# Metaformer block with routed experts: the last weight transfer in 80 and 5 partitions, and index searches in pairs ahead of the up products

## The chip, the cores and the metric

The kernel runs on one core of a Trainium2 chip. The metric is device time in microseconds of one execution; lower is better. The profile is one execution recorded by the hardware profiler. TensorE multiplies matrices, VectorE (DVE), ScalarE (ACT) and GpSimd (POOL) work elementwise, SyncE (SP) only issues transfers, as ScalarE and GpSimd do on the side.

## The reference, cut to what matters

```python
x = x + conv1x1(layernorm_over_channels(x), W)      # x: (16, 128, 16, 16), W from 32 reflections
t = tokens(x)                                       # 4096 tokens of 128 channels
xf = layernorm(t)
Sm = softmax(xf @ W_router + b_router)              # 32 experts
G_ek, idx_ek = top_k(Sm.T, 128)                     # each expert takes its 128 best tokens
tokens = xf[idx_ek]                                 # gather
act = silu(tokens @ W_up[group] + b_up[group])      # 8 groups of 4 experts, 341 columns
Eout = act @ W_down[expert] + b_down[expert]
y = zeros.at[idx_ek].add(G_ek[..., None] * Eout)    # scatter-add
x = from_tokens(t + y)
```

## The kernel before

**Front half.** The 4096 tokens are worked on in 8 chunks of 512 (`CH`), 4 tiles of 128 each. TensorE transposes and mixes, VectorE and ScalarE take the statistics, GpSimd scales the logits and the softmax. The normalised tokens `xf` and the softmax rows `S` are stored side by side in HBM as `token_rows`, the residual `x1` in a first accumulator `acc0`, and a second, `acc1`, is filled with zeros. Then each expert's threshold is searched and a 0/1 selection `sel` made of it, with prefix counts `cum`.

**Index searches.** `find(e)` (L1099) is one small TensorE product that picks, for the 128 slots of expert e, the rows of `cum` in which the slots' tokens lie. `token_number(e)` on VectorE (L904, L906) counts in this row and writes `idx[:, e]`. Two PSUM banks take turns, so `find(e)` waits for index e - 2. After every fourth index VectorE makes one more `onehot` (L898, L899). Eight searches (`FIRST_FINDS`) are made before the first up product. The other 24 are spread by two functions that say how many must have been made ahead of up product j of unit k and ahead of the down products of expert e: TensorE calls both, and VectorE follows the same order in its loop over the experts, where `find_up_to` and `while found < finds_before_down(e)` stand.

**Experts.** The 32 experts run in 9 units of 2, 2, 4, 4, 4, 4, 4, 4, 4. GpSimd gathers one expert's 128 rows with an indirect DMA (L493), as soon as its index is there and once all stores of `token_rows` and of both accumulators have landed. TensorE transposes a unit's rows (L1117), multiplies them with `wup` in three up products (L1129), ScalarE applies SiLU (L620), and TensorE multiplies with `wdn` (2 x 128 rows) and `wdn2` (85 rows and the bias) in three steps per expert (L1142). VectorE scales the result by the gate (L945). Order on TensorE: up(0), then for each unit k up(k + 1), the transposes of unit k + 2, down(k).

**Way back.** All gathers stand ahead of the scatters in GpSimd's queue, since `AHEAD = E`. The first 26 experts' outputs are scattered with adding DMAs (L502), alternately into `acc0` and `acc1`; each waits for the last one into the same accumulator. The last 6 experts (`ON_PE`) are added by TensorE instead: VectorE splits the outputs into three bf16 parts (L920 to L923) and makes a one-hot of the tokens (`hot`, L914), and 144 products (L1164) add them up in all eight PSUM banks. Then both accumulators are read back (L429 on SyncE's queue, L624 on ScalarE's), summed by VectorE (L953), transposed by TensorE into the same banks (L1169), copied by ScalarE (L627) and stored (L432).

**SyncE's queue**, in order: V, constants, x, more constants, `wup` (L400), `bup`, `wdn` in two transfers (L404), `wdn2` (L405), the down bias (L406), the zero fill of `acc1` (L410), then for each chunk the store of `x1` (L414) and of `S` (L417), the stores of `xf` (L423) in the order 0, 7, 1, 2, 3, 4, 6, 5, and after the first index the 1 MB load of the column numbers (L426).

Of the kernel before, what the change touches and what calls it, by code (L numbers as in the profile page):

```python
# [20 lines left out]
ROW = C + E  # L21
FF = [(0, 128), (128, 128), (256, DFF - 256)]
FR = DFF - 256
LEVELS = HH.bit_length() - 1
FLOOR = 2.0 ** -102

# [49 lines left out]


def finds_before_up(k, j):
    downed = UNITS[k - 1][0] if k else 0
    return min(E, FIRST_FINDS + downed + 3 * k + j + 1)  # L80


def finds_before_down(e):
    ups = 3 * min(UNIT_OF[e] + 2, len(UNITS))
    return min(E, FIRST_FINDS + e + ups + 1)


def constants():
# [32 lines left out]
def metaformer_block(nc, x, V, w_router, b_router, w_up, b_up, w_down, b_down, c32, c16, ch16, ccol, out):  # L121
# [7 lines left out]
    with ctx:  # L129
# [261 lines left out]
        @block.sync  # L391
        def _(sp):
            sp.dma_start(v_raw[:, :], V).then_inc(s_v, 16)
            sp.dma_start(k32[:, 0:2 * P], c32[:, 0:2 * P]).then_inc(s_const, 16)
            sp.dma_start(k32[:, 2 * P:C32_COLS], c32[:, 2 * P:C32_COLS]).then_inc(s_merge, 16)
            for g in range(CH):
                sp.dma_start(X[:, g, :].rearrange("p (u n) -> p u n", u=TPC), x_v[g // 2, g % 2]).then_inc(s_x[g], 16)
            sp.dma_start(k16[:, :], c16).then_inc(s_const16, 16)
            sp.dma_start(kh16[:, :], ch16).then_inc(s_const16, 16)
            sp.dma_start(wup[:, :, :], w_up.rearrange("g c f -> c g f")).then_inc(s_wup, 16)  # L400
            for j, (f0, fn) in enumerate(FF):
                sp.dma_start(bup[0:fn, j, :], b_up[f0:f0 + fn, :]).then_inc(s_bup, 16)
            for j in range(2):
                sp.dma_start(wdn[:, :, j, :], w_down[:, j * P:(j + 1) * P, :].rearrange("e f c -> f e c")).then_inc(s_wdn, 16)  # L404
            sp.dma_start(wdn2[0:FR, :, :], w_down[:, 2 * P:DFF, :].rearrange("e f c -> f e c")).then_inc(s_wdn, 16)  # L405
            sp.dma_start(wdn2[FR:FR + 1, :, :], b_down.rearrange("(o e) c -> o e c", o=1)).then_inc(s_wdn, 16)  # L406

            sp.wait_ge(s_zero, 1)
            for q in range(4):
                sp.dma_start(acc[1][q * 1024:(q + 1) * 1024, :].rearrange("(p k) c -> p (k c)", p=P), zero[:, :]).then_inc(s_acc1, 16)  # L410
            for g in range(CH + 2):
                if g < CH:
                    sp.wait_ge(s_x1, TPC * (g + 1))
                    sp.dma_start(acc_v[0][g], per_chunk(x1, g)).then_inc(s_acc0, 16)  # L414
                if g >= 2:
                    sp.wait_ge(s_S, g - 1)
                    sp.dma_start(rows_v[g - 2, :, :, C:ROW], per_chunk(S, g - 2)).then_inc(s_rows_s, 16)  # L417
            for g in (0, CH - 1, 1, 2, 3, 4, CH - 2, 5):
                if g < CH - 2:
                    sp.wait_ge(s_xf, g + 1)  # L420
                else:
                    sp.wait_ge(s_xfp, CH - g)
                sp.dma_start(rows_v[g, :, :, 0:C], per_chunk(xf, g)).then_inc(s_rows_x, 16)  # L423

            sp.wait_ge(s_idx, 1)
            sp.dma_start(columns, ccol.to_broadcast([P, TOK])).then_inc(s_col, 16)  # L426
            sp.wait_ge(s_sc[0], 16 * INTO.count(0))
            for g in range(CH):
                sp.dma_start(per_chunk(y0, g), acc_v[0][g]).then_inc(s_y[g], 16)  # L429
            for g in range(CH):  # L430
                sp.wait_ge(s_yo, g + 1)
                sp.dma_start(out_v[g // 2, g % 2], yo[:, g, :].rearrange("p (u n) -> p u n", u=TPC)).then_inc(s_out, 16)  # L432
            sp.wait_ge(s_out, 16 * CH)

        @block.gpsimd
        def _(pool):
# [73 lines left out]
            for e in range(AHEAD):  # L510
                gather(e)
            e = 0
            while AHEAD + 2 * e < E:
                scatter(e)
                gather(AHEAD + 2 * e)
                gather(AHEAD + 2 * e + 1)
                e += 1
            while e < SCATTERED:
                scatter(e)
                e += 1  # L520
# [435 lines left out]
        def _(pe):  # L956
# [146 lines left out]
            def find_up_to(n):  # L1103
                while finds[0] < n:
                    find(finds[0])
                    finds[0] += 1
# [24 lines left out]
            def down(k):  # L1131
                e0, n = UNITS[k]
                pe.wait_ge(s_act, 3 * (k + 1))
                for q in range(n):
                    e = e0 + q
                    find_up_to(finds_before_down(e))
                    if e >= 3:
                        pe.wait_ge(s_eo, e - 2)
                    for j in range(3):
                        w = wdn[:, e, j, :] if j < 2 else wdn2[:, e, :]  # L1140
                        rows_ = P if j < 2 else FR + 1
                        ins = mm(down_bank(e), act[0:rows_, k % 2, j, q * P:(q + 1) * P], w, start=(j == 0), stop=(j == 2))  # L1142
                    ins.then_inc(s_dn, 1)

            pe.wait_ge(s_wup, 16)
            pe.wait_ge(s_wdn, 64)
            gathered_transpose(0)
            up(0)
            gathered_transpose(1)
# [40 lines left out]
```

## Time and profile before

| | us |
|---|---|
| median of 3 runs | 200.35 |
| lowest and highest | 199.31, 201.8 |
| the profiled execution, as timed | 198.85 |
| its span, first to last instruction | 196.8 |

In the span TensorE's matmuls are busy 146.2 us (74%), weight loads 89.2, GpSimd 108.4 (55%), VectorE 91.1, ScalarE 71.0. About 2 us of the profiled execution lie outside its span. The mean granted TensorE clock is 0.809 of full speed. Busy shares are means over stages with different limits; what a stage waits for has to be read from its own stretch.

### The profile page before, as it was taken

Reading aid. Unit: us, or ns where it says so; the run is one execution under the profiler, and the core shown is the slowest. Engines: PE = TensorE matmul, PEld = TensorE weight load, DVE = VectorE, ACT = ScalarE, POOL = GpSimd, SP = SyncE. Lnnn points to the kernel's source line nnn. Section 1 sums busy time; section 2 is a strip of 40 time slices with the busy share of each in tenths; the row PEclk is TensorE's granted clock in tenths of the full one; section 3 lists DMA queues with packets and bytes.
Section 4 is the critical chain, followed back from the end, with each engine's and each line's share of the span. In section 5 each row is a group of like instructions: output and inputs, shape, how many; then the busy total and the mean of one; then the engine's idle time right before and its main releaser. Section 6 shows DMA issues by size and latency. Waiting matters only on the chain.

```text
span 196.8 us, 2406 instructions
## 1 busy us (share of the span) xinstructions
PE 146.2 (74%) x697; PEld 89.2 (45%) x697; DVE 91.1 (46%) x407; ACT 71.0 (36%) x241; POOL 108.4 (55%) x118
## 2 busy tenths in 40 slices
PE   1999965723126213995999699999975999999990
PEld 0557855611105101452357236776662344444590
DVE  2454998984774861322464513221299022200550
ACT  3266999437894500321233132345400000000161
POOL 2027479986460027773766557687788778730000
PEclk9999998555555555557599859999996699999999
DMA  4999994336989952221212122243414333369996
GB/s 98 301 336 308 289 292 120 82 81 214 393 252 263 330 217 67 67 70 33 66 51 67 33 70 32 27 40 27 40 17 40 27 27 34 35 113 328 395 284 189
DMA packets 33502, 28.31 MB, mean 144 GB/s; under 512 B 6800, under 2 KB 27216, under 8 KB 33360
## 3 DMA queue, kind: packets, MB, share of 16 engines
q1 hardware_dynamic: 26769, 21.70, 37.5%
q0 software_dynamic: 5280, 4.33, 15.3%
q10 hardware_dynamic: 1440, 2.13, 3.3%
q8 instruction: 6, 0.10, 0.2%
q14 instruction: 7, 0.06, 0.1%
HBM read 17.53 MB, written 10.62 MB: 143 GB/s over the span
## 4 chain that ended last, share of the span: by engine, by line
PE 37%; POOL 21%; issue 14%; DVE 12%; DMA 9%; ACT 3%; another core or an unknown queue 1%; SPq 0%; POOLq 0%; DVEq 0%; ACTq 0%
POOL acc L502 8%; PE PT L1129 7%; PE PZ L1142 6%; PE PM L1129 6%; POOL rs L463 4%; DMA x<-acc 3%; PE PM L1142 3%; POOL rs L456 3%; PE PT L969 3%; DMA acc<-X,idx 2%; PE PZ L1169 2%; PE PT L1117 2%; POOL act L469 2%; DVE wdn L914 2%; POOL act L466 2%
## 5 line engine op out<-in xcount | busy, mean ns | idle before, releaser
L502 POOL DMA_INDIRECT acc<-X,idx x26 | 43.4, 1669 | 11.5 <-issue 9.3
L493 POOL DMA_INDIRECT xg<-token_rows,idx x32 | 30.5, 954 | 31.4 <-DVE idx L906 23.2
L904 DVE TENSOR_SCALAR_CACHE_REDUCE junk<-PZ,k 128x128 f16<-128x128 f32 x32 | 11.1, 347 | 24.8 <-PE PZ L1099 14.6
L1017 PE MATMUL PZ<-stage_w,X 128*128 128x192 f32 x64 | 16.2, 410 | 6.3 <-DVE act L749 5.8
L1142 PE MATMUL PZ<-wdn,act 128*128 128x128 f32 x132 | 18.2, 281 | 1.0 <-DVE X L945 1.0
L627 ACT ACTIVATE X<-PZ 128x512 f32<-128x512 f32 x4 | 2.4, 597 | 45.2 <-PE PZ L1169 45.2
L1129 PE MATMUL PT<-xgT,wup 128*128 128x512 f32 (+3 forms) x28 | 18.2, 740 | 0.0
L620 ACT ACTIVATE act<-PT,bup 128x512 f32<-128x512 f32 (+3 forms) x14 | 9.0, 640 | 24.3 <-PE PT L1129 20.9
L1017 PEld LDWEIGHTS PZ<-stage_w,X 128*128 128x128 f32 x64 | 13.4, 238 | 8.2 <-DVE act L749 7.4
L1142 PEld LDWEIGHTS PZ<-wdn,act 128*128 128x128 f32 x132 | 16.0, 191 | 2.4 <-DVE X L945 1.4
L1129 PE MATMUL PM<-xgT,wup 128*128 128x512 f32 (+3 forms) x26 | 16.2, 714 | 0.0
L1164 PE MATMUL PZ<-wdn,S 128*128 128x512 bf16 x48 | 14.6, 410 | 2.1 <-DVE X L945 2.1
L1099 PE MATMUL PZ<-cum,onehot 32*128 32x129 f16 x32 | 8.0, 258 | 9.2 <-DVE idx L906 4.2
L945 DVE TENSOR_SCALAR X<-PZ,xg 128x128 f32<-128x128 f32 x22 | 7.6, 349 | 15.0 <-PE PZ L1142 12.5
L620 ACT ACTIVATE act<-PM,bup 128x512 f32<-128x512 f32 (+3 forms) x13 | 8.3, 636 | 16.7 <-PE PM L1129 13.6
L914 DVE TENSOR_SCALAR wdn<-wide,slot_token 128x4096 bf16<-128x4096 f16 x6 | 7.8, 1302 | 13.7 <-PE PZ L1164 13.7
L1099 PEld LDWEIGHTS PZ<-cum,onehot 32*128 32x128 f16 x32 | 3.0, 96 | 22.8 <-issue 16.2
L558 ACT ACTIVATE act<-act,mn 128x32 f32<-128x32 f32 x32 | 9.8, 309 | 5.8 <-DVE mn L753 5.8
L953 DVE TENSOR_TENSOR x<-x,xf 128x512 f32<-128x512 f32 x8 | 5.2, 692 | 14.3 <-DMA x<-acc 14.2
L712 DVE SCALAR_TENSOR_TENSOR x<-PZ,rs,xg 128x128 f32<-128x128 f32 x32 | 9.1, 347 | 4.0 <-PE PZ L1017 2.4
L1117 PE MATMUL PT<-k,xg 128*128 128x128 f32 x32 | 6.4, 328 | 5.5 <-DMA xg<-token_rows,idx 5.5
L1117 PEld LDWEIGHTS PT<-k,xg 128*128 128x128 f32 x32 | 5.1, 174 | 10.8 <-issue 10.8
(172 smaller groups left out, 280.5 us busy)
## 6 DMA issues: line engine op xcount, KB each, us to landing
X<-in_x SPq DMA_DIRECT2D x8, 256.0 KB, 5.2
acc<-zero SPq DMA_DIRECT2D x4, 512.0 KB, 5.2
acc<-x SPq DMA_DIRECT2D x8, 256.0 KB, 4.2
token_rows<-xf SPq DMA_DIRECT2D x8, 256.0 KB, 3.6
xf<-acc ACTq DMA_DIRECT2D x8, 256.0 KB, 5.7
x<-acc SPq DMA_DIRECT2D x8, 256.0 KB, 7.2
out<-X SPq DMA_DIRECT2D x8, 256.0 KB, 3.1
wup<-in_L_ffn_W_up SPq DMA_DIRECT2D x1, 1364.0 KB, 7.8
```

The costliest lines, as they stand in the source:

```text
L493: nc.gpsimd.indirect_dma_start(out=xg[:, e, :], out_offset=None, in_=rows[:, :], in_offset=bass.IndirectOffsetOnAxis(ap=idx[:, e:e + 1], a ...
L502: nc.gpsimd.indirect_dma_start(out=acc[i][:, :], out_offset=bass.IndirectOffsetOnAxis(ap=idx[:, e:e + 1], axis=0), in_=eo[:, e, :], in_off ...
L558: ins = nc.scalar.activation(pr[:, g, u, :], lg[:, g, u, :], ACT.Exp, bias=mn[:, g, u:u + 1], scale=-1.0, accum_out=sm[:, g, u:u + 1])
L620: nc.scalar.activation(act[0:fn, k % 2, j, 0:n * P], src, ACT.Silu, bias=bup[0:fn, j, e0 // PER:e0 // PER + 1]).then_inc(s_act, 1)
L904: link(nc.vector.tensor_scalar(junk2[:, :], PZ[:, e % 2, 0:P], c_("slot_col"), None, ALU.is_le, ALU.add, accum_out=below[:, e:e + 1]))
L914: nc.vector.tensor_scalar(hot(k), columns, slot_token[:, k:k + 1], None, ALU.is_equal).then_inc(s_hot, 1)
L1017: ins = mm(PZ[:, 2 * (g % 2) + u // 2, (u % 2) * W_:(u % 2 + 1) * W_], X[:, g, u * P:(u + 1) * P], stage_w[:, :], start=True, stop=True)
L1099: mm(PZ[:, e % 2, 0:P + 1], onehot[r, g, :], cum[r, g, 0:P + 1], start=True, stop=True).then_inc(s_find, 1)
L1117: ins = nc.tensor.transpose(PT[:, 0, q * P:(q + 1) * P], xg[:, e0 + q, 0:C], ident)
L1129: mm(dst, wup[:, e0 // PER, f0:f0 + fn], xgT[:, k % 2, 0:n * P], start=True, stop=True).then_inc(s_up, 1)
L1142: ins = mm(down_bank(e), act[0:rows_, k % 2, j, q * P:(q + 1) * P], w, start=(j == 0), stop=(j == 2))
L1164: ins = mm(out_bank(g), parts[j][:, k, :], hot(k)[:, g * 512:(g + 1) * 512], start=(k == 0 and j == 0), stop=False)
```

## The change

`wdn2`'s 85 weight rows are loaded by two DMAs, of 80 partitions and of 5, where there was one; the semaphore that TensorE waits for counts one DMA more. Ahead of each up product stand two searches (after the first eight, until all 32 are made, which is ahead of the last up product of unit 3), and none between down products; VectorE's order follows through the same function. A loop on GpSimd that ran no time with `AHEAD = E` is removed.

```diff
+FR_EVEN = FR // 16 * 16
...
 def finds_before_up(k, j):
-    downed = UNITS[k - 1][0] if k else 0
-    return min(E, FIRST_FINDS + downed + 3 * k + j + 1)
+    return min(E, FIRST_FINDS + 2 * (3 * k + j + 1))
 
 
 def finds_before_down(e):
-    ups = 3 * min(UNIT_OF[e] + 2, len(UNITS))
-    return min(E, FIRST_FINDS + e + ups + 1)
+    return min(E, FIRST_FINDS + 6 * min(UNIT_OF[e] + 2, len(UNITS)))
...
-            sp.dma_start(wdn2[0:FR, :, :], w_down[:, 2 * P:DFF, :].rearrange("e f c -> f e c")).then_inc(s_wdn, 16)
+            for f0, f1 in ((0, FR_EVEN), (FR_EVEN, FR)):
+                sp.dma_start(wdn2[f0:f1, :, :], w_down[:, 2 * P + f0:2 * P + f1, :].rearrange("e f c -> f e c")).then_inc(s_wdn, 16)
...
-            while AHEAD + 2 * e < E:
-                scatter(e)
-                gather(AHEAD + 2 * e)
-                gather(AHEAD + 2 * e + 1)
-                e += 1
...
                     e = e0 + q
-                    find_up_to(finds_before_down(e))
                     if e >= 3:
...
-            pe.wait_ge(s_wdn, 64)
+            pe.wait_ge(s_wdn, 80)
```

## Rows read from the trace of the kernel before

**Rows 1.** Chain that ended last, its end: start us, us, what.
```profile
172.81 4.47 DMA acc<-X,idx
177.30 6.68 DMA x<-acc
184.75 2.22 PE PZ L1169 x16
```

**Rows 2.** Timeline of GpSimd: start us, us, engine, line, what, [idle before <-releaser].
```profile
72.20 1.22 POOL L493 DMA_INDIRECT xg<-token_rows,idx  x1 [14.65 <-DVE idx L906]
...
118.54 0.94 POOL L493 DMA_INDIRECT xg<-token_rows,idx  x1 [1.82 <-DVE idx L906]
119.79 1.62 POOL L502 DMA_INDIRECT acc<-X,idx  x1 [0.30 <-issue]
```

**Rows 3.** Busy time by stretch: length, then engines, granted clock, DMA share, GB/s.
```profile
89.70:92.00 2.30, 0.04 (x1) 0.07 (x1) 0.52 (x3) 0.08 (x1) 0.00 (x0) 0.78 0.13 36
92.00:98.10 6.10, 6.10 (x9) 1.82 (x10) 2.95 (x16) 1.37 (x2) 4.28 (x5) 0.52 0.18 46
...
108.90:110.70 1.80, 0.04 (x1) 0.07 (x1) 0.96 (x6) 0.00 (x0) 0.00 (x0) 1.00 0.18 46
110.70:117.60 6.90, 6.90 (x14) 2.35 (x14) 2.21 (x14) 2.16 (x4) 4.71 (x5) 0.56 0.24 59
...
150.30:155.50 5.20, 5.15 (x13) 1.82 (x14) 2.04 (x4) 0.00 (x0) 3.96 (x3) 0.50 0.30 25
155.50:184.30 28.80, 28.80 (x133) 12.78 (x131) 4.26 (x4) 0.00 (x0) 15.21 (x9) 0.99 0.56 124
```

**Rows 4.** Timeline, ScalarE and VectorE after their pauses.
```profile
89.18 0.60 ACT L611 ACTIVATE xgT<-PT 128x512 f32<-128x512 f32 x1 [1.98 <-remote]
91.27 0.35 DVE L904 TENSOR_SCALAR_CACHE_REDUCE junk<-PZ,k 128x128 f16<-128x128 f32 x1 [5.06 <-remote]
...
109.71 0.35 DVE L945 TENSOR_SCALAR X<-PM,xg 128x128 f32<-128x128 f32 x1 [2.05 <-PE PZ L1142]
```

**Rows 5.** Timeline, the last chunks of xf (ScalarE), a one-hot and the first index (VectorE).
```profile
52.69 7.79 ACT L590 ACTIVATE xf<-x,shift,rs 128x128 f32<-128x128 f32 x20
...
66.83 0.35 DVE L899 SCALAR_TENSOR_TENSOR onehot<-k,bend,after 128x128 f16<-128x128 f16 x1
...
67.48 0.15 DVE L906 SCALAR_TENSOR_TENSOR idx<-below,PZ 128x1 int32<-128x1 f32 x1
```

**Rows 6.** Timeline of SyncE's queue: how long an issue held it.
```profile
20.59 8.07 SPq L405 DMA_DIRECT2D wdn<-in_L_ffn_W_down  x1
28.71 15.92 SPq L406 DMA_DIRECT2D wdn<-in_L_ffn_b_down  x1
...
61.34 5.81 SPq L423 DMA_DIRECT2D token_rows<-xf  x8
```

**Rows 7.** Busy time by stretch, for the DMA: last two columns, share and GB/s.
```profile
32.00:44.00 12.00, 6.49 (x19) 5.21 (x19) 11.01 (x70) 6.25 (x38) 10.96 (x20) 0.54 0.37 82
48.00:52.00 4.00, 1.00 (x6) 0.54 (x5) 2.24 (x8) 3.07 (x12) 2.44 (x3) 0.50 1.03 394
```

**Rows 8.** The page, DMA issues: KB each, median us from issue to landing.
```profile
token_rows<-xf SPq DMA_DIRECT2D x8, 256.0 KB, 3.6
...
wide<-in_const_columns SPq DMA_DIRECT2D x1, 1024.0 KB, 6.1
...
xg<-token_rows,idx POOLq DMA_INDIRECT x32, 2.7
```

**Rows 9.** Chain of waits: up and down products at the full clock.
```profile
100.92 1.05 PE PM L1129 x2
...
105.99 0.86 PE PM L1142 x6
107.01 0.86 PE PZ L1142 x6
...
118.86 1.34 PE PZ L1142 x12
```

## The prediction

> **What bounds the kernel now.** I read the chain of waits first, from its end [rows 1]: the last scatter (L502) is issued at 172.81 and lands 4.47 later, the y loads follow from 177.30 and take 6.68, VectorE sums the first chunk, and TensorE turns sums into output from 184.75 on. GpSimd's timeline [rows 2] shows where that end comes from. Its 32 gathers are issued from 72.20 to 118.54, its 26 scatters from 119.79 to 172.81 [rows 1, 2]. A scatter every (172.81 - 119.79) / 25 = 2.12 us is its steady pace, and a gather takes 0.94 + 0.30 of issue, about 1.25 us: 31 steps of that are 38.8 us, while it took 46.3. So 7.5 us of the gather stretch is waiting for indices, and all gathers stand ahead of the first scatter.
>
> The windows of TensorE [rows 3] show a second chain that ends at the same moment. From 150.30 to 184.30 it is busy without a gap (34 us) in the 144 token products (L1164), and only then do the sums reach it [rows 1]. So a gain on GpSimd alone buys nothing: both chains have to move, and the smaller move counts. Upstream on TensorE there are two holes, 89.70 to 92.00 and 108.90 to 110.70, and each is followed by a stretch at a granted clock of 0.5 (the 1.2 GHz level). The second hole is reopened by a search: VectorE got the product it waited for at 109.71 only, and in the first it came back at 91.27, after 5.06 us of idleness [rows 4].
>
> Both chains begin with the first gather. Its index is there at 67.63 (67.48 + 0.15) [rows 5], yet it starts at 72.20. GpSimd also waits there for the stores of xf into token_rows, which SyncE issued from 61.34 to 67.15 [rows 6], one behind the other. ScalarE had the last of these chunks ready at 60.48 [rows 5]. The SyncE queue was late: the transfer of 85 partitions at L405 and the small one behind it held it from 20.59 to 44.63 [rows 6]. From 32 to 44 the DMA engines moved 82 GB/s at a share of 0.37, and from 48 to 52, with ordinary transfers, 394 GB/s at 1.03 [rows 7]: the 85 partitions were spread over about a third of the engines.
>
> **The change part by part.** *The transfer in 80 and 5 partitions.* Nothing waits for wdn2 itself, its first reader is a down product, long after it has landed; what counts is the queue behind it. It is 85 x 32 x 512 B = 1.39 MB, 17 us at 82 GB/s. At the other rate of [rows 7] the 1.31 MB of 80 partitions take 3.3 us; twice that is my upper bound, since small packets may go slower. The 80 KB of the last 5 partitions take 1.0 us at the old rate. One more issue costs SyncE about 0.5 us. I expect 17 us to become 5 to 8, 6.5 as the middle, so SyncE is free about 10.5 us earlier, at 34 instead of 44.6. The fills and x1 stores then run while the channel statistics are computed, and the xf stores are no longer queued but go out as chunks come ready, the last at about 60.5. With 3.6 us to land [rows 8] it is there at 64 to 65, ahead of the index at 67.63. The first gather then waits for that index alone and starts at 67.9: 4.3 us earlier. Here the cover is 3 us thick; if it were gone, the start would move by less.
>
> The Trainium skill ("DMA: Bandwidth & Descriptors", section "Why a DMA increments its semaphore by 16 and not by 1") says that such a transfer uses the largest number of engines up to 16 that divides its outer size. That gives 5 for 85, 16 for 80, and 5 for the rest, and the share of 0.37 agrees. Its "Rules for kernel authors" say of two transfers to disjoint partition halves that they serialize and are not worth splitting; by that rule alone the queue would be no earlier, which is the second rival below.
>
> There is a new collision. The 1 MB load of the columns (L426) waits for index 0 and so starts just after 67.63 either way, and took 6.1 us to land; the first gathers now go out beside it, where they used to find it nearly done. A gather lands in 2.7 us [rows 8]. The second one, now issued at 69.4, lands at 72.1 undisturbed, and with the rest of that load (2.6 us at 394 GB/s) ahead of it at 73.8. I take 72.7, near the first since both are interleaved. Before, it was issued at 73.7 and landed at 76.4, and TensorE's first transpose waits for it, so TensorE's chain moves by 3.7 us (bounds 2.6 to 4.3).
>
> *Two searches ahead of each up product.* Before, 24 searches stand singly: one ahead of each of 15 up products and of 9 down groups. At the full clock a down group with a search takes 107.01 - 105.99 = 1.02 us, without one 1.34 / 2 = 0.67 [rows 9]: a lone search costs 0.35. Afterwards there are 12 pairs. The second of a pair costs at least 0 and at most another 0.35; I take 0.15, since it needs no switch of its own. 24 x 0.35 - 12 x 0.50 = 2.4 us at the full clock; as half of these places are at the low clock or hidden there, I take 1.5 us (bounds 0 and 3.1). VectorE must keep up: a search costs it 0.35 (L904 [rows 4]) and 0.15 (L906) and a short read between, so a pair about 1.1, and every second pair brings a one-hot (L899 takes 0.35 [rows 5], with its helper some 0.6). That is 1.4 on average. An up product at the full clock takes 1.05 [rows 9], with the pair ahead of it some 1.4 too: it fits, barely, and at the low clock easily.
>
> The indices now come in time for GpSimd. Index 31 is found in the 12th up product, about 97 to 99 us, and gather 31 at full pace goes out at 67.9 + 1.5 + 30 x 1.25 = 106.9. So the 7.5 us of waiting disappear, the first scatter starts at 108.2 instead of 119.8, and the last at 161.2 instead of 172.8. Experts' outputs are ready far ahead: those of the third unit were multiplied at 109.71 [rows 4]. GpSimd's chain moves by 11.6 us: 4.3 at the start, and 7.3 of the 7.5 (the first gather takes 0.3 longer than the others). Taking the gather loop's dead tail out changes no instruction.
>
> *No search between down products.* The hole at 108.90 was a search ahead of up product 12 that needed an index queued on VectorE behind the multiplications of the down results. After the change all searches are over by then, so its 1.8 us go, and with them the low clock after it. That price is seen at the late restart: 13 matmuls in 5.20 us against 133 in 28.80 [rows 3], 5.20 - 13 x 0.217 = 2.4 us. The hole at 89.70 is open: its releaser is not known to the profile ("remote"), ScalarE was held too, until 89.18 [rows 4], and the new order has all its searches done before the first down product, so VectorE's pause may be hidden, or fall inside the up products and be paid. Nothing (0) or 2.3 + 2.4 = 4.7 us is gained; the loss side is 2.7, the 5.06 us pause less the 2.3 already paid.
>
> **The sum.** TensorE: 3.7 + 1.5 + 1.8 + 2.4 = 9.4, plus 0.5 because the sums are there when it arrives, 9.9; with the first hole gone too, 14.6. GpSimd: 11.6. If TensorE gets ahead of GpSimd it idles 2 to 4 us before the sums, and the output stage starts at the low clock: 11.6 - 2.4 = 9.2. Both ways lead to about 9.5 us. The span of 196.8 becomes 187.3, the profiled execution's 198.85 becomes 189.35. The median of the runs, 200.35, lies 1.5 us above that execution, so the forecast is 200.35 - 9.5 = 190.85, say 190.9 us.
>
> **The rivals.** *Both holes come back, elsewhere.* For it: the first has no named releaser, so nothing shows that a search caused it. Against: all engines have more slack in the new order. TensorE then gains 3.7 + 1.5 + 0.5 = 5.7, and the time is 194.7. *The split does not free the queue*, because the two parts serialize or the b_down transfer behind them is what holds SyncE (L406 shows 15.92 us). Against it: that row is 16 KB and can only be waiting for what is ahead. The gather start stays at 72.2; the other terms give about 1.5 + 4.2 + 0.5 = 6.2 on TensorE and 7.3 on GpSimd, so 194.2. *Slower:* VectorE's pause of 5.06 us falls between two searches of a pair, TensorE idles in the middle of the up products, and the clock stays low through the up and down products after it, which were done at the full one. Each us of work at the full clock then costs another. Some 10 us of it would use up the gain, 14 us make the kernel slower by over 2%; 30 us of it would give over 215 us. Against it: the low stretches in [rows 3] are 5 to 7 us long, after holes of about 2 us. *More than forecast:* both holes vanish and the output stage starts at the full clock: 11.6, so 188.8.
>
> **How the numbers follow.** Forecast, 8 to 11 us saved: 0.58. The full 11.6: 0.10. Both holes: 0.16. Queue not freed: 0.07. Clock low, slower: 0.04. The remaining 0.05 is some wait not seen that eats most of the gain. A measurement of this kernel tells 2% from no change, 196.3 and 204.4. Forecast, full gain, both holes and queue lie below 196.3, 0.91 in all, of which I put 0.03 over the line for the scatter of the runs (199.31 to 201.8): 0.88 faster, 0.08 the same, 0.04 slower. The range reaches from the full gain, 188.8 less 0.8 of scatter, to the first rival's 194.7 plus as much: 188.0 to 195.5.
>
> **What would show it.** Right: L406 on the SyncE queue short and the fills starting near 34; the first gather at about 68; gathers every 1.25 us to about 107, with no wait for an index; the first scatter near 108; no TensorE hole before up product 12; the last scatter near 161; TensorE either unbroken into the output stage or idle for 2 to 4 us before it. Wrong: a first gather still after 70, gathers waiting for VectorE, a scatter pace above 2.3 us, or holes of over 2 us among the paired searches.

## The result, and the profile after

| | us |
|---|---|
| kernel before, median of 20 runs | 200.5 (199.25 to 204.23) |
| changed kernel, median of 20 runs | 201.42 (200.76 to 204.04) |
| ratio, 95% interval | 1.0075, 1.0049 to 1.0102 |
| profiled execution after: time, span, mean granted clock | 200.8, 198.5, 0.823 |

The change makes the kernel slower by 0.5 to 1.0%, where 190.9 was forecast. Some executions of any kernel fall into a slower state; here and below a ratio compares fast executions only, while a median is over all of them, so that the two can differ by 1%.

SyncE's queue, from its timeline in the changed kernel (start, how long it held the queue). The line numbers behind L404 are shifted: searches are L1094, up products L1124, transposes L1112, down products L1136, indices L899 and L901.

```profile
21.48 13.02 SPq L405 DMA_DIRECT2D wdn<-in_L_ffn_W_down  x2
34.54 0.32 SPq L406 DMA_DIRECT2D wdn<-in_L_ffn_b_down  x1
34.91 3.47 SPq L410 DMA_DIRECT2D acc<-zero  x4
...
52.55 9.18 SPq L423 DMA_DIRECT2D token_rows<-xf  x8
68.46 0.35 SPq L426 DMA_DIRECT2D wide<-in_const_columns  x1
```

L405 and L406 hold the queue until 34.86, where they held it until 44.63 [rows 6]. The stores of xf spread over 9.18 us since each waits for its chunk, and no longer queue behind one another.

GpSimd's timeline in the changed kernel:

```profile
69.36 1.22 POOL L493 DMA_INDIRECT xg<-token_rows,idx  x1 [10.95 <-DVE idx L901]
...
93.44 0.95 POOL L493 DMA_INDIRECT xg<-token_rows,idx  x1 [0.30 <-issue]
99.36 0.94 POOL L493 DMA_INDIRECT xg<-token_rows,idx  x1 [4.98 <-DVE idx L901]
...
108.86 0.94 POOL L493 DMA_INDIRECT xg<-token_rows,idx  x1 [2.33 <-DVE idx L901]
...
116.36 1.62 POOL L502 DMA_INDIRECT acc<-X,idx  x1 [0.30 <-issue]
```

The first gather is 2.84 us earlier than in [rows 2], and waits for the index alone. With it begins an unbroken run of twenty, one every 1.25 to 1.29 us after the first step, to 94.39. Then GpSimd waits twice for an index, 7.3 us in all: as much as before. The first scatter comes at 116.36, 3.4 us earlier than before, not 11.6.

ScalarE's and VectorE's timelines in the changed kernel, the idle time ahead of an instruction in brackets:

```profile
86.32 0.47 ACT L615 ACTIVATE act<-PT,bup 128x256 f32<-128x256 f32 x1 [3.78 <-PE PM L1124]
95.42 0.47 ACT L615 ACTIVATE act<-PM,bup 85x256 f32<-85x256 f32 x1 [8.62 <-remote]
97.56 0.60 ACT L606 ACTIVATE xgT<-PT 128x512 f32<-128x512 f32 x1 [1.68 <-remote]
...
118.84 0.69 ACT L615 ACTIVATE act<-PT,bup 128x512 f32<-128x512 f32 x1 [5.99 <-remote]
...
89.12 0.35 DVE L899 TENSOR_SCALAR_CACHE_REDUCE junk<-PZ,k 128x128 f16<-128x128 f32 x1 [4.37 <-remote]
```

And TensorE's:

```profile
81.66 1.22 PE L1124 MATMUL PT<-xgT,wup 128*128 128x256 f32 x2
83.48 0.27 PE L1094 MATMUL PZ<-cum,onehot 32*128 32x129 f16 x1 [0.60 <-issue]
...
85.09 1.15 PE L1124 MATMUL PM<-xgT,wup 128*85 128x256 f32 x2
86.04 1.06 PE L1112 MATMUL PT<-k,xg 128*128 128x128 f32 x4
86.89 2.76 PE L1136 MATMUL PZ<-wdn,act 128*128 128x128 f32 x12
98.22 0.36 PE L1094 MATMUL PZ<-cum,onehot 32*128 32x129 f16 x2 [8.56 <-ACT xgT L606]
...
119.58 1.09 PE L1124 MATMUL PT<-xgT,wup 128*85 128x512 f32 x2 [3.10 <-issue]
```

Set the two beside each other. The up product that ends at 82.88 is taken by ScalarE at 86.32; the one that ends at 86.24 at 95.42, 9.2 us later; the search of 83.48 is read by VectorE at 89.12, 5.4 us later. The transposes that end at 87.10 come last, at 97.56, 10.5 us later. ScalarE and VectorE were idle. By the profile TensorE's work was finished, but its readers went on only much later. I call such results late. The ends of matmuls are modelled in the profile, so it can't tell whether the product itself was late or only the word of it. The rows show that the delay grew from product to product (3.4, 5.4, 9.2, 10.5 us), and that the readers got the results in the order of TensorE's program. The releaser of four of the five waits in the first rows is put down to "remote", a source that the profile does not know, as in [rows 4]. TensorE runs ahead until it needs a copy of a late result, and then stands for 8.56 us.

The windows of the changed kernel, over both holes and the stretch between (columns as in rows 3):

```profile
89.65:98.22 8.57, 0.01 (x2) 0.01 (x1) 1.63 (x8) 1.07 (x2) 3.82 (x4) 0.50 0.19 48
98.22:104.60 6.38, 6.38 (x13) 1.99 (x14) 3.43 (x21) 1.37 (x2) 4.02 (x5) 0.52 0.15 39
116.50:119.58 3.08, 0.00 (x0) 0.00 (x0) 0.35 (x1) 0.74 (x2) 2.77 (x2) 1.00 0.34 48
```

Two holes are there again, and larger: 8.56 us against the first row of [rows 3], 3.08 against the third, though the second now stands ahead of the third up product of the unit, where it stood ahead of the first. The granted clock stays at its lower level (1.2 GHz) until about 104.6. In the end TensorE goes from its token products straight into the output stage at 187.16 (before: 184.75 [rows 1]), while the last scatter, at 169.66, is 3.15 us earlier than before. TensorE alone sets this end.

### The profile page after: what moved, and what is told of

The parts are those of the page before. It is cut to its first block, busy times and chain, and to the rows that moved or that the text cites. A ratio compares the mean times of both kernels' runs of the same rounds, so it can differ in the third digit from the quotient of the medians.

```text
span 198.5 us, 2410 instructions
## 1 busy us (share of the span) xinstructions
PE 139.5 (70%) x697; PEld 87.6 (44%) x697; DVE 91.0 (46%) x407; ACT 70.8 (36%) x241; POOL 109.2 (55%) x118
## 4 chain that ended last, share of the span: by engine, by line
PE 53%; POOL 13%; DVE 11%; issue 9%; another core or an unknown queue 5%; DMA 3%; ACT 3%; SPq 0%; POOLq 0%; DVEq 0%; ACTq 0%
PE PZ L1158 9%; PE PT L1124 7%; PE PZ L1136 6%; PE PM L1124 6%; PE PT L1158 4%; PE PM L1158 4%; POOL rs L463 4%; PE PM L1136 3%; POOL rs L456 3%; PE PT L964 2%; POOL act L469 2%; PE PZ L1163 2%; DVE wdn L909 2%; DMA k<-in_const_f 2%
## 5 line engine op out<-in xcount | busy, mean ns | idle before, releaser
L502 POOL DMA_INDIRECT acc<-X,idx x26 | 44.1, 1698 | 11.0 <-issue 7.5
L1012 PE MATMUL PZ<-stage_w,X 128*128 128x192 f32 x64 | 14.9, 385 | 6.9 <-DVE act L744 6.5
L1136 PE MATMUL PZ<-wdn,act 128*128 128x128 f32 x132 | 18.5, 289 | 1.0 <-DVE X L940 1.0
L1124 PE MATMUL PT<-xgT,wup 128*128 128x512 f32 (+3 forms) x28 | 17.0, 695 | 3.1 <-issue 3.1
L940 DVE TENSOR_SCALAR X<-PZ,xg 128x128 f32<-128x128 f32 x22 | 7.5, 349 | 23.1 <-PE PZ L1136 10.6
L1136 PEld LDWEIGHTS PZ<-wdn,act 128*128 128x128 f32 x132 | 17.2, 204 | 1.9 <-DVE X L940 1.4
L899 DVE TENSOR_SCALAR_CACHE_REDUCE junk<-PZ,k 128x128 f16<-128x128 f32 x32 | 11.1, 347 | 14.5 <-PE PZ L1094 7.3
L1094 PE MATMUL PZ<-cum,onehot 32*128 32x129 f16 x32 | 5.9, 263 | 16.7 <-ACT xgT L606 9.0
L1012 PEld LDWEIGHTS PZ<-stage_w,X 128*128 128x128 f32 x64 | 12.5, 226 | 8.3 <-DVE act L744 7.5
L1124 PE MATMUL PM<-xgT,wup 128*128 128x512 f32 (+3 forms) x26 | 15.2, 672 | 0.0
L1094 PEld LDWEIGHTS PZ<-cum,onehot 32*128 32x128 f16 x32 | 2.4, 97 | 26.5 <-issue 11.4
L463 POOL TENSOR_TENSOR rs<-ve,mhalf 128x4 f32<-128x4 f32 x8 | 8.1, 1006 | 4.0 <-DVE ve L729 4.0
L585 ACT ACTIVATE xf<-x,shift,rs 128x128 f32<-128x128 f32 x24 | 9.4, 482 | 0.0
L1003 PE MATMUL PM<-k,S 128*128 128x128 f32 x8 | 3.3, 408 | 8.4 <-ACT key L562 6.6
```

What stands on the lines that cost most here:

```text
L463: link(nc.gpsimd.tensor_tensor(rs2[:, g, :], ve2[:, g, :], mhalf[:, :], ALU.pow))
L502: nc.gpsimd.indirect_dma_start(out=acc[i][:, :], out_offset=bass.IndirectOffsetOnAxis(ap=idx[:, e:e + 1], axis=0), in_=eo[:, e, :], in_off ...
L585: ins = nc.scalar.activation(xf[:, t, :], x1[:, t, :], ACT.Identity, bias=shift2[:, g, u:u + 1], scale=rs2[:, g, u:u + 1])
L899: link(nc.vector.tensor_scalar(junk2[:, :], PZ[:, e % 2, 0:P], c_("slot_col"), None, ALU.is_le, ALU.add, accum_out=below[:, e:e + 1]))
L1012: ins = mm(PZ[:, 2 * (g % 2) + u // 2, (u % 2) * W_:(u % 2 + 1) * W_], X[:, g, u * P:(u + 1) * P], stage_w[:, :], start=True, stop=True)
L1124: mm(dst, wup[:, e0 // PER, f0:f0 + fn], xgT[:, k % 2, 0:n * P], start=True, stop=True).then_inc(s_up, 1)
```

## The experiments

The runs lay in five groups, each on another chip and at another time, so chip and time can't be told apart here. The kernel before took 200.36 us on chip A, 194.06 on B, 200.36 on C, 193.86 on D and 193.17 on E. Only kernels on one chip are set side by side; on which chip the runs of the result above lay is not known.

Two theories to begin with. **G**: a long unbroken run of indirect gathers on GpSimd makes TensorE's results late; before, waits for indices broke the run. **P**: the paired searches themselves stall TensorE and VectorE.

**The transfer alone** (chip A): the kernel before with only this.

```diff
-            sp.dma_start(wdn2[0:FR, :, :], ...
+            for f0, f1 in ((0, FR_EVEN), (FR_EVEN, FR)):
+                sp.dma_start(wdn2[f0:f1, :, :], ...
```

> The kernel before with the wdn2 transfer in 80 and 5 partitions, old order of the searches. Theory G (a long unbroken run of gathers holds back TensorE's results): the gathers start 3 us earlier, at 69.4, the indices come one per up product as before; the hole of 2.3 us near 90 stays or grows to 3 to 5 us, and the time is 197 to 200, a gain of 0.5 to 3 us. Theory P (the searches in pairs hold TensorE back): without pairs the hole is as before, the full shift of 2.8 us arrives, 197.5 to 198.

Measured: 197.1 us, ratio 0.9878 (0.9747 to 1.0009). ScalarE and TensorE at the first hole, from their timelines:

```profile
88.63 0.60 ACT L613 ACTIVATE xgT<-PT 128x512 f32<-128x512 f32 x1 [3.79 <-remote]
...
89.36 0.27 PE L1101 MATMUL PZ<-cum,onehot 32*128 32x129 f16 x1 [1.44 <-ACT xgT L613]
```

The first hole is 1.44 us. Here 14 gathers run from 68.74, then GpSimd waits 3.22 us for an index. But a second hole stands further on, larger than any of before:

```profile
120.94 0.69 ACT L622 ACTIVATE act<-PM,bup 128x512 f32<-128x512 f32 x1 [7.84 <-remote]
...
121.68 2.00 PE L1131 MATMUL PM<-xgT,wup 128*85 128x512 f32 x2 [4.60 <-ACT act L622]
```

ScalarE took at 120.94 an up product that ended at 116.22, behind seven unbroken gathers (107.33 to 115.79) and with two scatters already issued, at 116.09 and 118.02. Against the trace of before the first transpose starts 3.2 us earlier (73.25 and 76.47), but this execution, the slowest of the four, has only 1.0 us less span. The ratio stands for 2.4 us, and its interval just reaches no change.

**The order of the searches alone** (chip A).

```diff
-    return min(E, FIRST_FINDS + downed + 3 * k + j + 1)
+    return min(E, FIRST_FINDS + 2 * (3 * k + j + 1))
-    return min(E, FIRST_FINDS + e + ups + 1)
+    return min(E, FIRST_FINDS + 6 * min(UNIT_OF[e] + 2, len(UNITS)))
...
-                    find_up_to(finds_before_down(e))
```

> The kernel before with the new order of the searches, the transfer undivided; the gathers start at 72.2 as before and run without a break. Theory G: 20 gathers in one go, as in the changed kernel, so the same hole of about 8 us among the third unit's products, and 203 to 205, slower than before by the 2.8 us that the split brought to the changed kernel. Theory P: the same, so this run alone tells only whether the order and not the transfer makes the hole; if neither is right and the early transfers cause it, the hole is 2 us and the time 194 to 198.

Measured: 205.79 us, ratio 1.0353 (1.0205 to 1.0501). ScalarE's timeline:

```profile
87.29 0.47 ACT L618 ACTIVATE act<-PM,bup 128x256 f32<-128x256 f32 x1 [5.13 <-PE PT L1127]
94.38 0.47 ACT L618 ACTIVATE act<-PT,bup 128x256 f32<-128x256 f32 x1 [6.61 <-issue]
...
100.09 0.60 ACT L609 ACTIVATE xgT<-PT 128x512 f32<-128x512 f32 x1 [2.39 <-remote]
```

Late results again, behind 18 unbroken gathers (71.70 to 94.19). So the loss of the change is in the order: by the ratios the transfer gives 2.4 us (from a gain of 5.1 to a loss of 0.2) and the order costs 7.1 (4.1 to 10.0). The two together lost 0.9 to 1.8 us where results were late; the intervals are too wide to say whether the parts simply add. Both theories expect a loss here; the next runs tell them apart.

**Gathers of experts 8 to 31 left out** (chip A), so their rows hold what was in the buffer; the searches stay paired.

```diff
+GATHERED = 8
-            for e in range(AHEAD):
+            for e in range(GATHERED):
...
-                pe.wait_ge(s_g[k], 16 * n)
+                if e0 < GATHERED:
+                    pe.wait_ge(s_g[k], 16 * n)
```

> The changed kernel with the gathers of experts 8 to 31 left out (these experts multiply what lies in the buffer; all else is done). GpSimd is idle from about 80 on until the first scatter. Theory G: no late results on ScalarE and VectorE after 82, TensorE goes through the up and down products without the hole of 8.6 us and without the one of 3.1, and the clock comes back early; span 180 to 188. Theory P: the paired searches are all there, so the hole at 90 stays at 6 us or more.

Measured: 182.03 us. Windows of this kernel:

```profile
84.00:90.00 6.00, 6.00 (x25) 3.99 (x23) 2.79 (x16) 1.62 (x4) 3.10 (x2) 0.68 0.12 11
90.00:98.00 8.00, 7.92 (x43) 4.74 (x43) 4.86 (x29) 4.20 (x7) 3.17 (x3) 1.00 0.28 25
```

TensorE has no hole, with every pair of searches in place. P falls. This is one execution, and its time is no gain, since 24 gathers are missing.

**Gathers held until unit k - 2 is transposed** (chip A), which breaks the run by real waits.

```diff
             for e in range(AHEAD):
+                if UNIT_OF[e] >= 3:
+                    pool.wait_ge(s_gTs, UNIT_OF[e] - 1)
                 gather(e)
```

> The changed kernel, but the gathers of unit k (from the fourth unit on) wait until unit k - 2 has been transposed, which breaks their run into bursts of four. Theory G: the hole shrinks from 8.6 us to under 3, and the time is 190 to 197. Theory P: pacing changes nothing for TensorE, the hole stays, and the gathers end later: 201 to 205.

Measured: 200.26 us, ratio 0.9988 (0.9914 to 1.0062). GpSimd and ScalarE, from their timelines in the profiled execution, the fastest of ten at 197.34:

```profile
79.96 0.94 POOL L495 DMA_INDIRECT xg<-token_rows,idx  x1 [1.33 <-ACT xgT L608]
...
87.21 0.94 POOL L495 DMA_INDIRECT xg<-token_rows,idx  x1 [2.55 <-ACT xgT L608]
...
106.21 0.94 POOL L495 DMA_INDIRECT xg<-token_rows,idx  x1 [2.48 <-ACT xgT L608]
...
116.31 0.69 ACT L617 ACTIVATE act<-PT,bup 128x512 f32<-128x512 f32 x1 [5.48 <-remote]
```

With runs of 8, 4, 4, 4, 4 gathers the first hole is gone (ScalarE never idle over 2.2 us up to 90). But the pace is lost in waits, and the last eight gathers, 106.21 to 116.27 and almost unbroken, bring late results back. A run of eight at 68.62 had brought none, so no fixed number of gathers explains it.

**Plain transfers in place of gathers, from GpSimd's and from SyncE's queue** (chip B): experts 8 to 31 get fixed rows, as many bytes, so their tokens are other ones.

```diff
-                gather(e)
+                if e < 8:
+                    gather(e)
+                else:
+                    pool.wait_ge(s_idx, e + 1)
+                    nc.gpsimd.dma_start(xg[:, e, :], rows[e * P:(e + 1) * P, :]).then_inc(...)
```

> The changed kernel, but the rows of experts 8 to 31 are fetched from GpSimd's queue by plain transfers of the same 82 KB each, at fixed rows, when the index is ready (what these experts multiply is not what the reference asks for; the amount is the same). If it is the bytes landing in the buffer that hold TensorE's results back, the hole stays at 6 to 9 us. If it is the run of indirect issues on GpSimd, it goes or shrinks under 3 us, and the span is 182 to 190.

> As the run with plain transfers from GpSimd, but issued by SyncE, so GpSimd stands idle from the eighth gather to the first scatter, and the bytes still land in the same buffer. Bytes: hole of 6 us or more, span over 193. GpSimd's issues: no hole, span 178 to 184, as with the gathers left out (179.9).

Measured: 181.9 and 181.51 us, neither with a hole. I first read this as "not the bytes, but the gathers". Then the next two ran beside them, and the reading had to wait.

**Fewer gathers ahead** (chip B): the changed kernel with the old loop back and at work, 16 or 12 gathers, then a scatter and two gathers in turn.

```diff
-AHEAD = E
+AHEAD = 16
...
+            while AHEAD + 2 * e < E:
+                scatter(e)
+                gather(AHEAD + 2 * e)
+                gather(AHEAD + 2 * e + 1)
+                e += 1
```

> The changed kernel with the loop put to use: 16 gathers ahead, then a scatter and two gathers in turn. A scatter with its two gathers takes about 1.85 + 2.5 = 4.35 us. The first 16 gathers are one run (as long as in the kernel before), so a hole of 2 to 4 us near 90 is expected by the theory of the run's length; after it none. GpSimd: 68.7 + 20 + 8 x 4.35 + 18 x 2.1 = 161 for the last scatter, 9 earlier than in the changed kernel. Time 188 to 195. If mixing with scatters does not relieve TensorE, holes of 5 us or more among units 4 to 7 and 198 or more.

> The same with 12 gathers ahead and ten alternations. The run is shorter, the hole near 86 under 2 us. The third unit's successors are fetched later: unit 8's last rows at 68.7 + 15 + 10 x 4.35 = 127, about when TensorE would want them; last scatter about 161. Time 187 to 194, at best 2 us under the variant with 16.

Measured: 16 ahead 189.38 us, ratio 0.9829 (0.9705 to 0.9953); 12 ahead 194.61, ratio 1.0064 (1.0019 to 1.0109). With 12, TensorE waits five more times for a gather after its first (0.8 to 2.9 us). But with 16 there was no late result even within the first 16 gathers, which are the same stream, at nearly the same times, as in the changed kernel, where results were late from 83 on. G as first stated cannot say that, and on this chip the kernel before was 6 us faster too. All further kernels ran beside the changed kernel itself.

**The same on a chip with late results** (C): the changed kernel again, plain transfers again (24 experts with other rows), 16 ahead again.

> The changed kernel itself, as the control for the runs beside it, since two groups of earlier runs lay on chips on which the kernel before took 200.4 and 194.1 us. If how late TensorE's results arrive depends on the chip, then on a chip where the kernel before takes about 194 this one shows no idle stretch of ScalarE over 3 us between 80 and 98, no hole of TensorE over 2 us there, and takes 189 to 192. On a chip with 200 for the kernel before it shows the 6 to 9 us hole again and takes 200 to 202. If the run of gathers alone makes the hole, whatever the chip, the hole is there on either.

> Experts 8 to 31 are fetched by plain transfers of fixed rows from GpSimd's queue, so the output is another one. Theory G (the run of indirect gathers holds TensorE's results back): no idle stretch of ScalarE over 3 us from a late result, about 182 us, on the same chip on which the changed kernel beside it shows its hole. If it was the chip that made the earlier run of this kernel look clean, then on a chip where the changed kernel shows the hole this one shows it too, and takes 188 to 190.

> The changed kernel with the old loop at work, AHEAD = 16: 16 gathers, then a scatter and two gathers in turn; repeated beside the changed kernel, since it was run on another chip before. Theory G: at most 3 us of late results in the run of the first 16, none later, and 7 to 11 us less than the changed kernel beside it on a chip where that one shows its hole. If the gain of the earlier run came from the chip, it is within 3 us of the changed kernel here.

Measured: the changed kernel 202.2 us, ratio 1.0091 (1.0043 to 1.0139); plain transfers 183.75; 16 ahead 194.49, ratio 0.9702 (0.9654 to 0.9749). ScalarE's timeline in the changed kernel on this chip, then the same stretch of windows with it and with plain transfers:

```profile
84.78 0.47 ACT L615 ACTIVATE act<-PM,bup 128x256 f32<-128x256 f32 x1 [4.89 <-PE PT L1124]
93.21 0.47 ACT L615 ACTIVATE act<-PT,bup 128x256 f32<-128x256 f32 x1 [7.95 <-remote]
```

```profile
84.00:90.00 6.00, 1.32 (x5) 0.79 (x5) 1.03 (x6) 0.47 (x1) 4.48 (x6) 0.50 0.24 63
```

```profile
84.00:90.00 6.00, 5.93 (x25) 4.01 (x23) 3.24 (x18) 1.75 (x3) 3.16 (x7) 0.75 0.28 80
```

TensorE is busy 1.32 of 6 us with gathers and 5.93 with plain transfers, on one chip. So it is the indirect gathers, and not the bytes, now with a control beside it. It is one execution, and the two kinds differ in more than the indices: twelve plain transfers hold GpSimd for 6.52 us, 0.54 each, where a gather holds it for 0.95 and goes out every 1.25, and the plain ones wait again for indices from 85.8 on (2.81, 1.97 us). Which of these matters is not separated. Nor is the whole gain one of late results, since on chip B, without any, plain transfers took 181.9 us. With 16 ahead, GpSimd and ScalarE:

```profile
88.58 0.95 POOL L493 DMA_INDIRECT xg<-token_rows,idx  x1 [0.31 <-issue]
94.36 1.62 POOL L502 DMA_INDIRECT acc<-X,idx  x1 [4.84 <-DVE X L945]
...
85.17 0.47 ACT L620 ACTIVATE act<-PM,bup 128x256 f32<-128x256 f32 x1 [4.98 <-PE PT L1129]
92.22 0.47 ACT L620 ACTIVATE act<-PT,bup 128x256 f32<-128x256 f32 x1 [6.58 <-PE PM L1129]
```

Results are late in the first run, and the last of them arrive at 92.22, 2.7 us after its last gather left GpSimd at 89.53. In the turns of a scatter and two gathers that follow there is no late result any more. That is where the gain of 3.9% over the changed kernel (0.9702 to 1.0091) comes from: a first stretch that ends 1 us sooner (92.22 against 93.21), no second one, and earlier scatters. I had expected at most 3 us of late results in the first run; it was 4.98 and 6.58.

**A break by work, and the control** (chips D and E): after the tenth gather GpSimd writes zeros over zeros four times.

```diff
             for e in range(AHEAD):
+                if e == 10:
+                    for _ in range(4):
+                        link(nc.gpsimd.memset(zero[:, :], 0.0))
                 gather(e)
```

> The changed kernel with one break in its run of 20 gathers: after the tenth, GpSimd writes zeros four times over a buffer that holds zeros (0.95 us each and a wait, 4 to 4.5 us in all), then goes on. Theory G, a long unbroken run of indirect gathers makes TensorE's results late: what is late at 84 to 85 arrives as soon as the break comes (81.5 to 86), the idle stretch of 8 us that ends at 93 to 95 shrinks to under 4, and the kernel takes 3 to 6 us less than the changed kernel beside it. Rival, it is how many gathers there are in all and not that they are unbroken: idle stretches of 5 and 8 us as in the changed kernel, shifted by up to 4 us, and 0 to 4 us more than it.

> The changed kernel itself, the control for the three runs beside it. On a chip where the kernel before takes about 200: 201 to 203 us, ScalarE idle for 8 to 9 us up to 93 to 96. On one where it takes about 194: if the chip sets how late results come, the idle stretches of ScalarE stay under 3 us and it takes 189 to 193; if the order alone sets it, they are 5 and 8 us here too.

> The changed kernel with the break of four writes of zeros (1.35 us each with its wait, 5.3 us in all) after the tenth gather, again, since the chip of the first try showed no late results at all. On a chip where the kernel before takes about 200: theory G, what is late arrives in the break, the 8 us idle stretch of ScalarE shrinks to under 4 and the kernel takes 3 to 6 us less than the changed kernel beside it; the rival (the number of gathers, broken or not) keeps stretches of 5 and 8 us and 0 to 5 us more. On a chip with about 194: no late results with or without, and 3 to 5 us more than the changed kernel, as the first time (194.46 beside 190.21).

> The changed kernel itself, the control. If the chips are of two kinds: 201 to 203 us with stretches of 5 and 8 us of late results where the kernel before takes about 200; 189 to 191 us and none where it takes about 194, with the first gather at 68.5, the gathers unbroken to 107.6 and the first scatter at 108.8.

Measured: with the break 194.46 us on D and 194.27 on E; the changed kernel 190.21, ratio 0.9827 (0.9748 to 0.9906), and 190.33, ratio 0.9874 (0.9762 to 0.9986). Neither chip has late results, so the break shows only what it costs (the first scatter is 4.5 us later on D and 3.9 on E), and whether it would make late results arrive sooner is open. The find is the control: on these chips **the same change is a gain of 1.3 to 1.7%**, and both intervals stay below 1. The changed kernel on E, GpSimd and TensorE:

```profile
68.80 1.22 POOL L493 DMA_INDIRECT xg<-token_rows,idx  x1 [10.94 <-DVE idx L901]
...
107.87 0.95 POOL L493 DMA_INDIRECT xg<-token_rows,idx  x1 [0.30 <-issue]
109.12 1.62 POOL L502 DMA_INDIRECT acc<-X,idx  x1 [0.30 <-issue]
...
161.78 1.55 POOL L502 DMA_INDIRECT acc<-X,idx  x1 [0.67 <-DMA acc<-X,idx]
...
73.22 0.66 PE L1112 MATMUL PT<-k,xg 128*128 128x128 f32 x2 [2.02 <-DMA xg<-token_rows,idx]
...
173.46 3.78 PE L1163 MATMUL PZ<-k,x 128*128 128x128 f32 x16 [4.44 <-DVE x L948]
```

All 32 gathers run unbroken, and nothing is late.

**The kernel before, on such a chip** (E).

> The kernel before itself, with a profile, for the same. If late results are a trait of the chip, then on a chip with about 194 it has neither ScalarE's idle stretch ended by an unknown source at 89 nor the 5 us of VectorE at 91, no hole of TensorE of 2 us at 90, but still the hole that a search makes at 109 to 111, which comes from the order. On a chip with about 200 it shows the rows of before once more.

Measured: 193.93 us, span 191.8. GpSimd and TensorE, and the windows:

```profile
72.36 1.22 POOL L493 DMA_INDIRECT xg<-token_rows,idx  x1 [14.74 <-DVE idx L906]
...
115.61 1.62 POOL L502 DMA_INDIRECT acc<-X,idx  x1 [0.30 <-DVE X L945]
...
168.79 1.55 POOL L502 DMA_INDIRECT acc<-X,idx  x1 [0.31 <-issue]
...
76.59 0.66 PE L1117 MATMUL PT<-k,xg 128*128 128x128 f32 x2 [5.55 <-DMA xg<-token_rows,idx]
...
179.22 2.41 PE L1169 MATMUL PZ<-k,x 128*128 128x128 f32 x16 [0.96 <-DVE x L953]
```

```profile
84.00:90.00 6.00, 6.00 (x21) 3.87 (x21) 2.18 (x12) 2.02 (x4) 4.73 (x5) 0.50 0.29 71
...
108.00:112.00 4.00, 4.00 (x15) 1.59 (x14) 2.03 (x13) 1.37 (x2) 2.99 (x4) 1.00 0.26 66
```

Neither hole is there. I had expected the one at 109 to 111 to stay, as made by a search. It doesn't: both holes of [rows 3] came with late results. The trace of before shows it of the second one as well:

```profile
105.92 0.94 PE L1142 MATMUL PM<-wdn,act 128*128 128x128 f32 x6
```

This product ends at 106.86, and VectorE, idle before, takes it at 109.71 [rows 4], 2.9 us later; the search that reopens the hole then waits for an index behind it.

**20 ahead, and 16 ahead with the old order of searches** (chip D).

```diff
-AHEAD = E
+AHEAD = 20
```

> The changed kernel with AHEAD = 20: 20 gathers, then a scatter and two gathers in turn. Theory G: the first 20 gathers are the same unbroken run as in the changed kernel, so the first late stretch is there (8 us, on a chip with 200 for the kernel before), 2 to 3 us more of it than with 16 ahead; no second hole at 116 to 119, since scatters break the runs behind it; GpSimd waits for no index. 3 to 5 us less than the changed kernel, and 2 to 4 us more than with 16 ahead (0.970 of the kernel before), so a ratio of 0.98 to 0.99. If the gain with 16 ahead came only from starting the scatters early, the two are alike, 0.965 to 0.975.

> The kernel before with the transfer split and AHEAD = 16, and its own order of searches: are the paired searches worth anything once the gathers are broken up? If lone searches cost 0.35 us each and pairs 0.5, as in my sum, it takes 1 to 3 us more than the changed kernel with AHEAD = 16, a ratio of 0.975 to 0.985. If the order of the searches matters only by when the indices let gathers go, its indices come later, the run of gathers is broken earlier, and it is as fast or faster: 0.96 to 0.972.

Measured: 20 ahead 190.64 us (186.81 to 192.53); old order, split transfer and 16 ahead 189.91, ratio 0.9812 (0.9742 to 0.9883). With the changed kernel at 190.21 beside them these are alike: where nothing is late, how far the gathers run ahead and how the searches are spread hardly matter. What I expected of 20 ahead was for a chip with late results, and stays open.

## Why the prediction was wrong, point by point

**What bounds the kernel.** Two chains with one end, both begun by the first gather: right, on both kinds of chip. What I read wrongly is the 7.5 us that GpSimd waited for indices. On chip E the kernel before waits only (114.35 - 72.36) - 31 x 1.25 = 3.2 us, its last gather being at 114.35. The other 4.3 us came with late results: TensorE stood, so searches came late, so indices came late. I took an effect for a cause.

**The transfer.** Right. The queue is free at 34.86, 9.8 us earlier, where 34 and 10.5 were forecast. Queue time from L405 to L406 went from 24.0 to 13.4 us [rows 6]. The Trainium skill's rule ("DMA: Bandwidth & Descriptors", "Rules for kernel authors") that two transfers to disjoint partition halves are not worth splitting does not hold for this one, of 80 and 5 partitions, as these 10.6 us show. The first gather came at 69.36, forecast 67.9: GpSimd started 0.9 us after its index and the front half ran 0.8 us later in this execution. The first transpose moved by 76.47 - 73.68 = 2.8 us, inside the bounds of 2.6 to 4.3 though not the 3.7 of the sum. Chip E gives 76.59 - 73.22 = 3.4.

**The searches.** That VectorE keeps up and nothing stalls in a pair: right, since on chips D and E TensorE has no gap over 0.7 us between the first up products and the token products. That the indices come in time: right there, with the last gather at 107.87, forecast 106.9, and the first scatter at 109.12, forecast 108.2.

**The step that failed** is "all engines have more slack in the new order", said against the rival of both holes coming back, and the sum behind it, which costed an unbroken run of gathers at nothing to TensorE. In the profiled execution of the result the run of 20 gathers makes results late by up to 10.5 us. The first hole grew by 8.56 - 2.3 = 6.3 us and the second by 3.1 - 1.8 = 1.3, where I had the second gone (1.8 + 2.4) and the first unchanged. With the 2.8 us of the earlier start that is +4.8; +2.4 was measured at the start of the output stage; how the difference splits between fewer lone searches and the clock was not measured. The warning was in [rows 4]: a releaser called "remote", and ScalarE and VectorE held at the same time. I named the gap and then asked only whether searches would fall into it, not what made it. My rival of both holes coming back (194.7 us) came nearest in mechanism, but let them keep their size, while they grew by 7.6 us in all. My slower rival had the right sign and the wrong mechanism: VectorE's pause inside a pair, where it was the gathers' run, which kept results from both engines.

**Where nothing is late**, the forecast was 9.5 and 4.1 us of span came (191.8 to 187.7 on E, one execution of each kernel; the medians there, 193.17 and 190.33, lie 2.8 apart). By its own terms, the sum being that of the two rows above it:

| GpSimd's chain and the end | forecast | chip E |
|---|---|---|
| start of the first gather | 4.3 | 72.36 - 68.80 = 3.6 |
| waits for indices that go | 7.3 | 6.5 - 3.6 = 2.9 |
| last scatter | 11.6 | 168.79 - 161.78 = 7.0 |
| start of the output stage | 11.6 | 179.22 - 173.46 = 5.8 |
| output stage at the low clock | -2.4 | (187.7 - 173.46) - (191.8 - 179.22) = -1.7 |
| sum | 9.2 | 4.1 |

TensorE idled 4.44 us before the output stage (forecast 2 to 4), its token products ending 178.26 - 169.02 = 9.2 us earlier (forecast 9.4). So the shape was right, and the term most off is the 7.3, of which 2.9 came: again the index waits that had come in part with late results. The 190.9 us forecast lie close to the 190.3 measured there, but by chance: the kernel before took 193.2 and not 200.4.

## What to carry to other kernels

A wait that looks like pure loss can be a brake that something else lives on: before costing its removal as a gain, ask what the engine behind it will then do at full pace, and whom that disturbs. An idle time that ends by an unknown releaser on two engines at once is a mechanism still to be found, not a hole to be filled. And compare kernels on one chip, with the changed kernel beside every variant: 16 gathers ahead, then a scatter and two gathers in turn, gave 0.970 of the kernel before on a chip with late results, where the changed kernel gave 1.009, and 0.983 on one without, where the changed kernel gave 0.983 to 0.987 on two others of its kind.

## What the runs showed of the hardware

- TensorE's results reached ScalarE and VectorE 3 to 10 us after their modelled ends, in order, while GpSimd issued indirect gathers one every 1.25 us. In the changed kernel some came within the run and the last 3.2 us after its last gather left (94.39, 97.56); with 16 ahead on chip C the last came 2.7 us after (89.53, 92.22). Plain transfers of the same bytes from the same queue did nothing of the kind on the same chip, in one execution. What inside the chip does it was not found, nor whether the product or only the word of it is late.
- Loading of code does not explain it: in the changed kernel's trace no packet of the two instruction queues moves between 80.5 and 114.6, and the readers went on at 95.42 and 97.56 all the same.
- It appeared on chips A and C and not on B (seen there with 16 ahead), D and E, with the same instructions. The kernel before takes 200.4 us on the first two and 193.2 to 194.1 on the others. Whether this is the chip or its condition at the time is open.
- Two gathers between scatters brought nothing late on chip C. But scatters alone do not end it at once: with the transfer alone, on chip A, a result came at 120.94, behind scatters issued at 116.09 and 118.02. Waits break the run (first hole, chip A). That a break by work on GpSimd does was not seen, as neither try met a chip with late results.
